# Cross-attention and spectral FFN, one core: one more product per slot from step 56, two blocks' outputs moved, the last context normalised in halves

## The chip, the cores and the metric

The kernel runs on one core of a Trainium2 chip. The metric is the device time of one execution in microseconds (us), median of several runs. Every length of an operation below comes from one profiled execution; times inside it are microseconds from the start of its span.

## The reference

Two batches of 2048 tokens, model width 512, 16 heads of 32, 128 keys of context per batch. What is computed:

```python
q, k, v = decoder_output @ wq_w + wq_b, encoder_output @ wk_w + wk_b, encoder_output @ wv_w + wv_b
score = einsum('bhqd,bhkd->bhqk', q, k) / sqrt(KEY_SIZE) * mask
score = where(score == 0, -1e9, score)
context = softmax(score) @ v                       # heads joined again
x = x + (context @ wo_w + wo_b)                    # q from layernorm(x)
x = x + real(ifft(fft(layernorm(x)) @ w)) + bias   # w complex; here one real 512 x 512 matrix
```

## The kernel before, in words

The 4096 tokens are 16 blocks (c = 0 to 15) of 256 tokens, each of two tiles (t = 0, 1) of 128. All the attention work of a block is cut into four steps s = 4c to 4c+3 of four heads each, 64 steps in all. Weights, queries, contexts and normalised rows are split into a high and a low fp16 part (names ending in h and l), so each 512-wide product is 12 matmuls of 512 columns (high by high, high by low, low by high, four slices each).

Every engine runs one hand-ordered list, and the lists are cut into **slots** v. `plan()` (top of the file) makes TensorE's list. In slot v TensorE (PE) does:

- PT(v-2): the probabilities of step v-2 are transposed (`turn`, L641; 8 transposes, buffers `bank2`, `bank3`), after ScalarE has finished their exponentials (`ex_done`);
- the "mid" products of the slot; WO(c,t) is the attention's output product of tile t of block c (L478, operands `ch`, `cl`), FF(c,t) the FFN product of that tile (L478, operands `x1h`, `x1l`, for block 15 `lasth`, `lastl`);
- S(v+1): the scores of step v+1 (`scores`, L627), which may overwrite the one pair of score banks only when VectorE has read step v (`tt_done`);
- in odd slots PV((v-3)/2): context of two steps (`weigh`, L655); in even ones R((v-4)/2), a "late" fill: the spread reciprocals are turned (L584), after GpSimd's `spread` (L1250, tile `rzb`, semaphore `p_rz`); late products too.

The fills use three PSUM banks in turn (`G[n % 3]`), so a fill waits until VectorE has freed the bank of the third fill before it (`g_free`).

VectorE (DVE) per slot: `mask_mul(v)` (L961, scores times mask), in odd slots `ctx_norm` (L986, context times reciprocal, tile `cn`), `zero_to_neg(v)` (L968, both inputs in SBUF, `eq_done`), `least(v)` (L973, minima), then `lo(n)` for the products: `x <- bank` (L940 after WO, with `bn_stats` L1036 and `bn_aggr` L1041 behind it; L946 after FF). ScalarE (ACT) per slot: in odd slots `copy_rec` (L760, waits for R) first, then half of the exponentials of step v-1 (`exps`, L744, waits for `nbias`), `copy_pt(v-2)` (L753), the other half, and in odd slots `ctx_hi` (L767, `ch` from `cn`). GpSimd (POOL) per slot: it waits for `eq_done` of the slot, then low parts of normalised rows (`norm_lo2`, L1218, `x1nl`), `bias(v)` (L1243, `nbias`, needs `least(v)`; the exponentials wait for it), `ctx_lo` (L1256, `cl`, needs `ch`), `spread` (L1250), `add_bf` (L1229), `add_bo` (L1195), and for blocks 12 and 13 also `norm_hi2` (L1212, `x1nh`), which needs the tile's WO drained by VectorE. `rstd2` (L1202, L1205) is the root for a tile.

FF(c,t) needs `x1h` and `x1l`: the rows `x1nh`, `x1nl` transposed by two DMAs that SyncE (SP) issues (`turn_x1n`, L396) after `p_l2`, the signal of `norm_lo2`. For block 13, tile 1, `norm_lo2` stands in slot 63, ahead of `bias(63)` and behind the wait for `eq_done` of step 63.

After step 63 there is no more softmax: PT63, R30, R31 and PV31 finish block 15's context, `last_ctx_lo` makes its low part, then WO(15,0), WO(15,1), FF(14,0), FF(14,1), FF(15,0), FF(15,1) run (the last in two halves of 256 columns), VectorE adds each, SP stores.

Of the kernel before, what the change touches and what calls it, by code (L numbers as in the profile page):

```python
# [37 lines left out]
def plan():  # L38
# [22 lines left out]
    for v in range(V0, V1):  # L61
# [8 lines left out]
        mid = {NS - 4: [("FF", NC - 4, 0)], NS - 3: [("WO", NC - 3, 1)], NS - 2: [], NS - 1: [("FF", NC - 3, 0)],  # L70
               NS: [("WO", NC - 2, 0)], NS + 1: [("WO", NC - 2, 1)], NS + 2: [("FF", NC - 3, 1)], NS + 3: []}.get(v, mid)
# [57 lines left out]
def build(nc, x, xt, ctx_in, mask, wq, bq, wk, bk, wv, bv, wo, bo, lparts, tables, bf, eye, sums, pick, places, heads, out):  # L129
# [3 lines left out]
    with ExitStack() as stack:  # L133
# [133 lines left out]
        p_l1, p_l2, p_zero, last_cl = (sem(n) for n in ("p_l1", "p_l2", "p_zero", "last_cl"))  # L267
# [410 lines left out]
        def _(act):  # L678
# [136 lines left out]
            for v in range(V0, V1):  # L815
# [55 lines left out]
                if r == 2 and 0 <= c - 2 < NC and v != NS + 2 and c - 2 not in (0, 12, 13):  # L871
                    norm_hi2(c - 2, 1)
                for a in range(4, NC):
                    if hi_slot(a) == v:
                        split_hi(a)
        @block.vector
        def _(dve):
# [207 lines left out]
            for v in range(V0, V1):  # L1085
# [44 lines left out]
                if v == NS - 1:  # L1130
                    tasks += [(stats2, mean2, NC - 3, t) for t in range(2)]
                for n in held + mids:
                    if fills[n][0] == "WO" and fills[n][1] != NC - 3:
# [20 lines left out]
        def _(pool):  # L1154
# [397 lines left out]
```

## Time and profile before

| | us |
|---|---|
| median of 3 runs | 437.13 (437.1 to 437.85) |
| the profiled execution's own time | 437.16 |
| its span, first to last instruction | 435.4 |
| PE busy in the span | 429.1 |
| DVE busy | 398.4 |
| ACT busy | 365.1 |
| POOL busy | 355.6 |
| PE's granted clock | 1.000 of full speed |

The span is what the profile shows; 1.8 us of the execution lie around it. A matmul's row gives its latency (0.38 us for 512 columns), and matmuls of one group start 0.216 us apart, so PE can count as busy while it waits a little: waits are better read from start to start.

### The profile page before, as it was taken

To read this page: it belongs to the slowest core of one execution; us is meant where nothing else is said; L and a number is where in the kernel's file an instruction comes from. 1 tells how busy PE (TensorE), PEld (TensorE's weight loads), DVE (VectorE), ACT (ScalarE), POOL (GpSimd) and SP (SyncE) were. 2 spreads that over 40 slices of the span, in tenths; PEclk is the share of its full clock that TensorE was granted. 3 is DMA by queue.
4 is the path that set the end of the run, shared out by engine and by line. 5 is a ranking of instruction groups with operands and counts; after the bars stand their busy time and mean duration, and the time that the engine had idled before them with its cause. 6 is when DMAs were issued, how large, how long until landed. Compare 5 with 4: busy or idle time off the path is not lost.

```text
span 435.4 us, 10922 instructions
## 1 busy us (share of the span) xinstructions
PE 429.1 (99%) x3496; PEld 297.3 (68%) x3496; DVE 398.4 (92%) x533; ACT 365.1 (84%) x1340; POOL 355.6 (82%) x484
## 2 busy tenths in 40 slices
PE   7999999999999999999999999999999999999997
PEld 6897788686776676666677667766676765556544
DVE  3899799999999999999999999999999899999663
ACT  1768997889988998999898998998998899999720
POOL 5779988868999898989889898989899865665693
PEclk9999999999999999999999999999999999999999
DMA  8999954404545655445454545445542434331144
GB/s 269 396 387 256 305 167 125 107 0 110 128 108 123 168 95 161 102 124 140 128 147 130 132 112 153 92 136 145 110 104 63 108 79 112 75 88 49 50 110 132
DMA packets 85286, 60.15 MB, mean 138 GB/s; under 512 B 40141, under 2 KB 72813, under 8 KB 84718
## 3 DMA queue, kind: packets, MB, share of 16 engines
q1 hardware_dynamic: 84508, 59.29, 50.0%
q8 instruction: 29, 0.48, 0.5%
q10 hardware_dynamic: 722, 0.17, 0.2%
q14 instruction: 27, 0.22, 0.2%
HBM read 29.33 MB, written 8.39 MB: 87 GB/s over the span
## 4 chain that ended last, share of the span: by engine, by line
PE 90%; DVE 4%; POOL 2%; issue 2%; ACT 1%; POOLq 0%; DVEq 0%
PE bank L478 34%; PE bank L483 24%; PE bank L641 11%; PE bank L655 6%; PE scores L627 5%; PE bank L584 3%; PE bank L565 2%; PE scores L483 1%; DVE zs L968 1%; ACT zs L744 1%; PE bank L661 1%; PE bank L491 1%; DVE zs L961 1%; POOL cl L1256 1%; DVE x L946 0%
## 5 line engine op out<-in xcount | busy, mean ns | idle before, releaser
L744 ACT ACTIVATE zs<-zs,nbias 128x128 f32<-128x128 f32 x512 | 199.8, 397 | 13.9 <-POOL nbias L1243 13.5
L744 ACT ACTIVATION_READ_ACCUMULATOR zs<-zs,nbias 128x1 f32 x512 | 99.5, 194 | 0.0
L968 DVE SCALAR_TENSOR_TENSOR zs<-zs 128x1024 f32<-128x1024 f32 x64 | 89.0, 1390 | 1.1
L973 DVE TENSOR_REDUCE nmin<-zs 128x8 f32<-128x1024 f32 x64 | 78.1, 1220 | 2.1
L961 DVE TENSOR_TENSOR zs<-scores,ms 128x1024 f32<-128x1024 f32 x64 | 78.0, 1218 | 0.1
L753 ACT COPY pt<-bank 128x512 f32<-128x512 f32 x128 | 67.9, 582 | 8.2 <-PE bank L641 8.0
L641 PE MATMUL bank<-ident,zs 128*128 128x128 f32 x512 | 66.7, 273 | 0.1
L1195 POOL TENSOR_TENSOR xs<-xs,bob 128x512 f32<-128x512 f32 (+1 forms) x41 | 43.4, 1059 | 22.9 <-DVE zs L968 22.8
L483 PE MATMUL bank<-xth,wqh 128*128 128x256 f16 x224 | 61.2, 273 | 0.0
L483 PE MATMUL bank<-xtl,wqh 128*128 128x256 f16 x224 | 61.1, 273 | 0.0
L483 PE MATMUL bank<-xth,wql 128*128 128x256 f16 x224 | 61.1, 273 | 0.0
L641 PEld LDWEIGHTS bank<-ident,zs 128*128 128x128 f32 x512 | 57.6, 140 | 3.6 <-ACT zs L744 1.7
L478 PE MATMUL bank<-woh,ch 128*128 128x512 f16 x128 | 48.5, 379 | 0.9 <-POOL cl L1256 0.6
L478 PE MATMUL bank<-wol,ch 128*128 128x512 f16 x128 | 48.5, 379 | 0.0
L478 PE MATMUL bank<-woh,cl 128*128 128x512 f16 x128 | 48.5, 379 | 0.0
L478 PE MATMUL bank<-mh,x1h 128*128 128x512 f16 x120 | 45.5, 379 | 0.0
L478 PE MATMUL bank<-ml,x1h 128*128 128x512 f16 x120 | 45.5, 379 | 0.0
L478 PE MATMUL bank<-mh,x1l 128*128 128x512 f16 x120 | 45.5, 379 | 0.0
L1218 POOL TENSOR_TENSOR x1nl<-x,x1nh 128x512 f16<-128x512 f32 x30 | 35.8, 1195 | 9.8 <-DVE zs L968 9.6
L1229 POOL TENSOR_TENSOR x<-x,bfb 128x512 f32<-128x512 f32 x32 | 41.2, 1288 | 1.2 <-DVE zs L968 1.2
L1250 POOL COPY rzb<-rz 128x512 f32<-128x512 f32 x32 | 38.5, 1204 | 2.9 <-DVE rz L979 2.6
L627 PEld LDWEIGHTS scores<-ks,qs 102*128 102x128 f16 (+1 forms) x480 | 31.9, 97 | 13.2 <-issue 0.2
(128 smaller groups left out, 903.9 us busy)
## 6 DMA issues: line engine op xcount, KB each, us to landing
xs<-in_x SPq DMA_DIRECT2D x16, 512.0 KB, 4.3
xtr<-in_xt SPq DMA_DIRECT2D x16, 512.0 KB, 4.6
out<-x SPq DMA_DIRECT2D x31, 256.0 KB, 2.5
qs<-qh SPq DMA_DIRECT2D x120, 64.0 KB
lp<-in_lparts SPq DMA_DIRECT2D x4, 1024.0 KB, 10.3
qs<-ql SPq DMA_DIRECT2D x60, 64.0 KB
ms<-in_mask SPq DMA_DIRECT2D x16, 128.0 KB, 2.5
wks<-in_wk SPq DMA_DIRECT2D x2, 512.0 KB, 6.5
```

Source lines behind the costliest of these rows:

```text
L478: last = pe.matmul(o, a, b, start=(i == 0), stop=(i == len(mm) - 1))
L483: last = pe.matmul(o, a, b, start=(first and i == 0), stop=(i == len(pairs) - 1))
L627: last = pe.matmul(A[:, n % 2, 128 * j:128 * j + 128], qs[c % 2][0:rows, g, j, 128 * t:128 * t + 128], ks[0:rows, g, j, c // (NC // NB), : ...
L641: last = pe.transpose(PB[f][:, a:a + 128], zs[:, s % NZ, t, 2 * f + i, :], ident[:])
L744: last = act.activation(z, z, ACT.Exp, bias=nbias[:, s % 4, i:i + 1], scale=-NEG, accum_out=zsum[:, s % 4, i:i + 1])
L753: act.copy(pt[:, s % 2, 2 * f:2 * f + 2, :], PB[f][:]).then_inc(pt_copied, 1)
L961: dve.tensor_tensor(zs[:, s % NZ], A[:].rearrange("p t (h k) -> p t h k", h=4), ms[:, c % NM].unsqueeze(2).broadcast_to([128, 2, 4, KEYS]) ...
L968: dve.scalar_tensor_tensor(out=z, in0=z, scalar=0.0, in1=z, op0=ALU.is_equal, op1=ALU.subtract).then_inc(eq_done, 1)
L973: dve.tensor_reduce(nmin[:, s % 4, :], zs[:, s % NZ].rearrange("p t h k -> p (t h) k"), AX.X, ALU.min).then_inc(mn_done, 1)
L1195: i = pool.tensor_tensor(z, z, bob[:, n], ALU.add)
L1229: pool.tensor_tensor(z, z, bfb[:], ALU.add).then_inc(p_x1b, 1)
L1250: pool.tensor_copy(rzb[:].rearrange("p i h w -> p (i h) w"), rz[:, z, :].rearrange("p i h -> p (i h)").unsqueeze(2).broadcast_to([128, 16, ...
```

## The change

In the table of mid products (rows 4 of the slots around the end) and in the lists of POOL, DVE and ACT:

- FF(11,0) moves from slot 58 to 56, FF(11,1) from 59 to 58, FF(12,0) from 60 to 59; WO(12,0) becomes a late fill of slot 56. So slot 56 has two products, and slot 60 one less.
- FF(12,1) moves from the end of slot 62 ahead of the scores there. FF(13,1) moves from slot 66 to 64. WO(14,0) moves from 64 to 65, WO(14,1) from 65 to 66. WO(13,0) stays behind the scores of slot 60.
- In the slots 58, 59, 62 and 63 (`BEHIND`) DVE drains the slot's products one slot later, behind the next `least`.
- POOL: block 12's `norm_hi2` and statistics are done as block 13's were; in slot 61 `norm_hi2(13,0)` now stands ahead of `bias(61)`.
- The last context is normalised, cast and subtracted in two halves of 128 tokens (`last_ctx_norm`, `last_ctx_hi`, `last_ctx_lo`; semaphores `last_cn`, `last_ch`, `last_cl`), so WO(15,0) waits for the first half only.

Counts of matmuls, transposes and DMAs are the same.

```diff
+BEHIND = (NS - 6, NS - 5, NS - 2, NS - 1)
...
-        mid = {NS - 4: [("FF", NC - 4, 0)], NS - 3: [("WO", NC - 3, 1)], NS - 2: [], NS - 1: [("FF", NC - 3, 0)],
-               NS: [("WO", NC - 2, 0)], NS + 1: [("WO", NC - 2, 1)], NS + 2: [("FF", NC - 3, 1)], NS + 3: []}.get(v, mid)
+        mid = {NS - 8: [("FF", NC - 5, 0)], NS - 6: [("FF", NC - 5, 1)], NS - 5: [("FF", NC - 4, 0)],
+               NS - 2: [("FF", NC - 4, 1)], NS - 1: [("FF", NC - 3, 0)], NS: [("FF", NC - 3, 1)],
+               NS - 4: [], NS + 1: [("WO", NC - 2, 0)], NS + 2: [("WO", NC - 2, 1)], NS + 3: []}.get(v, mid)
...
-        if v == NS - 4:
-            late.append(("WO", NC - 3, 0))
-        if v == NS - 2:
-            late.append(("FF", NC - 4, 1))
+        if v in (NS - 8, NS - 4):
+            late.append(("WO", v // 4 - 2, 0))
...
+        first = [n for n in held if fills[n][0] in ("R", "ST") and v - 1 not in BEHIND]
+        slots[v] = (items, first, [n for n in held if n not in first],
+                    [n for n in mids if fills[n][0] != "R" and v not in BEHIND])
+        held = mids + lates if v in BEHIND else lates
...
-                    pe.wait_ge(ch_done, 2 * c + 2)
+                    pe.wait_ge(ch_done, min(2 * c + 2, NS // 2 - 1))
                     pe.wait_ge(p_cl, min(2 * c + 2, NS // 2 - 1))
                     if c == NC - 1:
-                        pe.wait_ge(last_cl, 1)
+                        pe.wait_ge(last_ch, f + 1)
+                        pe.wait_ge(last_cl, f + 1)
...
+            def last_ctx_hi():
+                c = NC - 1
+                act.wait_ge(g_done, at["WO", c - 2, 1] + 1)
+                for t in range(2):
+                    g = slice(128 * t, 128 * t + 128)
+                    act.wait_ge(last_cn, t + 1)
+                    act.copy(ch[:, c % 2, 2:4, g], cn[:, :, g]).then_inc(last_ch, 1)
...
                 if v == NS + 1:
+                    copy_rec(NS // 2 - 1)
                     norm_hi2(NC - 2, 0)
-                    copy_rec(NS // 2 - 1)
-                    norm_hi2(NC - 2, 1)
-                    ctx_hi(NS // 2 - 1)
+                    last_ctx_hi()
...
+                if v == NS - 5:
+                    rstd2(NC - 4, 0)
+                    rstd2(NC - 4, 1)
...
-                if v == 57:
+                if v == 61:
                     norm_hi2(c - 2, 0)
                 if 0 <= v < NS:
                     bias(v)
...
-                if v == NS - 3:
+                if v == NS - 7:
                     norm_hi2(c - 2, 0)
-                    spread((v - 3) // 2)
+                if v in (NS - 7, NS - 3):
                     norm_lo2(c - 2, 0)
```

**Place 1: PE's list around slots 58 to 60.** Eleven more matmuls of each product are left out. `ident,zs` is PT, `pt,vs` is PV, `ident,rzb` is R, `mh,x1h` opens an FF, `woh,ch` a WO. Before, from PT56 to WO(13,0):

```order
L641 MATMUL bank<-ident,zs 128x128 x8
L478 MATMUL bank<-mh,x1h 128x512
...
L627 MATMUL scores<-ks,qs_63 128x128 x8
L584 MATMUL bank<-ident,rzb 128x128 x4
L641 MATMUL bank<-ident,zs 128x128 x8
L478 MATMUL bank<-mh,x1h 128x512
...
L627 MATMUL scores<-ks,qs_64 128x128 x8
L655 MATMUL bank<-pt,vs 32x256 x8
L641 MATMUL bank<-ident,zs 128x128 x8
L478 MATMUL bank<-mh,x1h 128x512
...
L627 MATMUL scores<-ks,qs_64 128x128 x8
L584 MATMUL bank<-ident,rzb 128x128 x4
L478 MATMUL bank<-woh,ch 128x512
```

Now, slots 59 and 60, from PT57 to WO(13,0):

```order
L643 MATMUL bank<-ident,zs 128x128 x8
L479 MATMUL bank<-mh,x1h 128x512
...
L629 MATMUL scores<-ks,qs_64 128x128 x8
L657 MATMUL bank<-pt,vs 32x256 x8
L643 MATMUL bank<-ident,zs 128x128 x8
L629 MATMUL scores<-ks,qs_64 128x128 x8
L585 MATMUL bank<-ident,rzb 128x128 x4
L479 MATMUL bank<-woh,ch 128x512
```

The product between PT58 and the scores of step 61 is gone, so S61 and R28 come right behind PT58.

**Place 2: PE's list from PV30 to the product behind PV31.** Before:

```order
L655 MATMUL bank<-pt,vs 32x256 x8
L641 MATMUL bank<-ident,zs 128x128 x8
L478 MATMUL bank<-woh,ch 128x512
...
L584 MATMUL bank<-ident,rzb 128x128 x4
L641 MATMUL bank<-ident,zs 128x128 x8
L478 MATMUL bank<-woh,ch 128x512
...
L584 MATMUL bank<-ident,rzb 128x128 x4
L655 MATMUL bank<-pt,vs 32x256 x8
L478 MATMUL bank<-mh,x1h 128x512
```

Now:

```order
L657 MATMUL bank<-pt,vs 32x256 x8
L643 MATMUL bank<-ident,zs 128x128 x8
L479 MATMUL bank<-mh,x1h 128x512
...
L585 MATMUL bank<-ident,rzb 128x128 x4
L643 MATMUL bank<-ident,zs 128x128 x8
L479 MATMUL bank<-woh,ch 128x512
...
L585 MATMUL bank<-ident,rzb 128x128 x4
L657 MATMUL bank<-pt,vs 32x256 x8
L479 MATMUL bank<-woh,ch 128x512
```

FF(13,1) stood last of these, behind PV31; it is now the first product behind PT62.

**Place 3: POOL's list, slot 61.** Before:

```order
L1243 TENSOR_SCALAR nbias<-nmin 128x8
L1212 CAST x1nh<-x_76 128x512
L1250 COPY rzb<-rz 128x512
L1218 TENSOR_TENSOR x1nl<-x_76,x1nh 128x512
L1256 TENSOR_TENSOR cl<-cn,ch 128x512
```

Now:

```order
L1231 CAST x1nh<-x_76 128x512
L1262 TENSOR_SCALAR nbias<-nmin 128x8
L1237 TENSOR_TENSOR x1nl<-x_76,x1nh 128x512
L1269 COPY rzb<-rz 128x512
L1275 TENSOR_TENSOR cl<-cn,ch 128x512
```

The cast of tile (13,0), which waits for the drain of WO(13,0), is now ahead of `nbias` of step 61.

## Rows read from the trace of the kernel before

**Rows 1.** The page, busy time, share, instructions, all engines.

```profile
PE 429.1 (99%) x3496; PEld 297.3 (68%) x3496; DVE 398.4 (92%) x533; ACT 365.1 (84%) x1340; POOL 355.6 (82%) x484
```

**Rows 2.** PE timeline, slots 56 to 58: start, us, operation, [idle before, releaser].

```profile
363.67 1.09 PE L641 MATMUL bank<-ident,zs 128*128 128x128 f32 x8
365.39 0.38 PE L478 MATMUL bank<-woh,ch 128*128 128x512 f16 x1 [0.63 <-POOL cl L1256]
...
367.98 0.61 PE L627 MATMUL scores<-ks,qs 102*128 102x128 f16 x8
368.43 0.61 PE L584 MATMUL bank<-ident,rzb 128*128 128x128 f32 x4
368.87 1.04 PE L641 MATMUL bank<-ident,zs 128*128 128x128 f32 x8
369.75 0.38 PE L478 MATMUL bank<-woh,ch 128*128 128x512 f16 x1
...
372.33 0.61 PE L627 MATMUL scores<-ks,qs 102*128 102x128 f16 x8
372.88 1.07 PE L655 MATMUL bank<-pt,vs 128*32 128x256 f32 x16
373.88 1.09 PE L641 MATMUL bank<-ident,zs 128*128 128x128 f32 x8
```

**Rows 3.** PE timeline, places where starts lie further apart (slots 59, 65, 66).

```profile
377.85 0.60 PE L584 MATMUL bank<-ident,rzb 128*128 128x128 f32 x4
378.60 1.09 PE L641 MATMUL bank<-ident,zs 128*128 128x128 f32 x8
...
408.67 1.04 PE L641 MATMUL bank<-ident,zs 128*128 128x128 f32 x8
409.87 0.39 PE L478 MATMUL bank<-woh,ch 128*128 128x512 f16 x1 [0.17 <-DVE x L946]
...
416.39 0.38 PE L478 MATMUL bank<-mh,x1l 128*128 128x512 f16 x1
416.89 0.38 PE L478 MATMUL bank<-woh,ch 128*128 128x512 f16 x1
```

**Rows 4.** DVE timeline, step 63's `zero_to_neg`.

```profile
400.58 1.55 DVE L968 SCALAR_TENSOR_TENSOR zs<-zs 128x1024 f32<-128x1024 f32 x1
```

**Rows 5.** POOL and SP timelines behind it, and landings of `x1l` there.

```profile
402.28 1.16 POOL L1218 TENSOR_TENSOR x1nl<-x,x1nh 128x512 f16<-128x512 f32 x1 [1.23 <-DVE zs L968]
...
404.75 1.26 SPq L396 DMA_TRANSPOSE x1l<-x1nl  x1
...
DMA to landing us min/median/max: 2.5/2.5/2.5
```

**Rows 6.** ACT timeline, slot 59 before.

```profile
381.08 1.04 ACT L753 COPY pt<-bank 128x512 f32<-128x512 f32 x2
...
383.58 0.61 ACT L767 CAST ch<-cn 128x512 f16<-128x512 f32 x1
```

**Rows 7.** DVE timeline, slot 59 and the start of 60.

```profile
380.88 0.68 DVE L986 TENSOR_TENSOR cn<-bank,rec 128x512 f32<-128x512 f32 x1
381.48 1.22 DVE L968 SCALAR_TENSOR_TENSOR zs<-zs 128x1024 f32<-128x1024 f32 x1
382.74 1.22 DVE L973 TENSOR_REDUCE nmin<-zs 128x8 f32<-128x1024 f32 x1
383.87 0.74 DVE L946 SCALAR_TENSOR_TENSOR x<-bank,rs,x 128x512 f32<-128x512 f32 x1
...
384.69 1.16 DVE L961 TENSOR_TENSOR zs<-scores,ms 128x1024 f32<-128x1024 f32 x1
```

**Rows 8.** DVE and POOL timeline, `zero_to_neg` meeting POOL's operations.

```profile
198.19 0.73 POOL L1195 TENSOR_TENSOR xs<-xs,bob 128x256 f32<-128x256 f32 x1
198.33 1.67 DVE L968 SCALAR_TENSOR_TENSOR zs<-zs 128x1024 f32<-128x1024 f32 x1
198.85 1.62 POOL L1250 COPY rzb<-rz 128x512 f32<-128x512 f32 x1
```

More of the change, by code:

```diff
@@ L265, in build @@
         dc_done, wz_lo, l0_done, m_hi, m_lo, b_zero, l2_done, o_lo = (sem(n) for n in ("dc_done", "wz_lo", "l0_done", "m_hi", "m_lo", "b_zero", "l2_done", "o_lo"))
[L267 removed]
+        p_l1, p_l2, p_zero, last_cn, last_ch, last_cl = (sem(n) for n in ("p_l1", "p_l2", "p_zero", "last_cn", "last_ch", "last_cl"))
         p_const, p_ms, p_nb, p_cl, p_st, p_xb, p_r2, p_x1b, p_sm, l_done, p_rz = (
@@ L872, in _ @@
                     norm_hi2(c - 2, 1)
+                if v == NS + 2:
+                    norm_hi2(NC - 2, 1)
                 for a in range(4, NC):
@@ L986, in ctx_norm, with last_ctx_norm @@
                 dve.tensor_tensor(cn[:], CX[:].rearrange("p (i n) -> p i n", i=2), rec[:], ALU.mult).then_inc(cn_done, 1)
+            def last_ctx_norm():
+                m = NS // 2 - 1
+                dve.wait_ge(rc_done, m + 1)
+                dve.wait_ge(pv_done, m + 1)
+                dve.wait_ge(p_cl, m)
+                for t in range(2):
+                    g = slice(128 * t, 128 * t + 128)
+                    dve.tensor_tensor(cn[:, :, g], CX[:].rearrange("p (i n) -> p i n", i=2)[:, :, g], rec[:, :, g],
+                                      ALU.mult).then_inc(last_cn, 1)
             def last_ctx_lo():
-                m = NS // 2 - 1
                 c = NC - 1
-                dve.wait_ge(ch_done, m + 1)
-                dve.tensor_tensor(cl[:, c % 2, 2:4, :], cn[:], ch[:, c % 2, 2:4, :], ALU.subtract).then_inc(last_cl, 1)
+                for t in range(2):
+                    g = slice(128 * t, 128 * t + 128)
+                    dve.wait_ge(last_ch, t + 1)
+                    dve.tensor_tensor(cl[:, c % 2, 2:4, g], cn[:, :, g], ch[:, c % 2, 2:4, g],
+                                      ALU.subtract).then_inc(last_cl, 1)
             def split_lo0():
@@ L1119, in _ @@
                         recip(0)
-                    if fills[n][0] not in ("M", "Y") and v != NS - 1:
+                    if fills[n][0] not in ("M", "Y"):
                         lo(n)
@@ L1129, in _ @@
                           if a != 6 and stats_slot(a, t) == v]
[L1130 to L1133, printed above, removed]
+                if v in (NS - 6, NS - 1):
+                    tasks += [(stats2, mean2, NC - 4 + (v == NS - 1), t) for t in range(2)]
+                for n in mids:
+                    if fills[n][0] == "WO" and fills[n][1] not in (NC - 4, NC - 3):
                         tasks.append((stats2, mean2, *fills[n][1:]))
@@ L1136, in _ @@
                     stats(*ct)
-                if v > 3 and v % 2 == 1 and 0 <= v - 3 < NS - 2 and v not in (NS - 3, NS - 1):
+                if v > 3 and v % 2 == 1 and 0 <= v - 3 < NS - 2:
                     recip((v - 3) // 2)
@@ L1330, in _ @@
                     add_bo(15, 0)
-                if r == 1 and 0 <= c - 2 < NC and v not in (13, NS - 3, NS + 1):
+                if r == 1 and 0 <= c - 2 < NC and v not in (13, NS - 7, NS - 3, NS + 1):
                     rstd2(c - 2, 0)
+                if v == NS - 5:
+                    rstd2(NC - 4, 0)
+                    rstd2(NC - 4, 1)
                 if v == NS:
                     rstd2(NC - 3, 0)
-                    rstd2(NC - 3, 1)
                 if v == NS + 2:
@@ L1339, in _ @@
                     rstd2(1, 0)
-                if r == 2 and 0 <= c - 2 < NC and v not in (NS - 2, NS + 2):
+                if r == 2 and 0 <= c - 2 < NC and v not in (NS - 6, NS - 2, NS + 2):
                     rstd2(c - 2, 1)
@@ L1421, in _ @@
                     norm_lo2(c - 2, 1)
-                if v not in (NS - 4, NS + 1) and r < 2 and 0 <= c - 3 < NC and v > 13 and not (r == 1 and VT <= v < NS):
+                if v not in (NS - 8, NS - 4, NS + 1) and r < 2 and 0 <= c - 3 < NC and v > 13 and not (r == 1 and VT <= v < NS):
                     add_bf(c - 3, r)
@@ L1427, in _ @@
                     norm_hi2(c - 2, 1)
+                if v == 56:
+                    add_bo(13, 1)
                 if v == 60:
@@ L1430, in _ @@
                     add_bo(14, 1)
+                if v == NS:
+                    rstd2(NC - 3, 1)
+                    add_bf(NC - 3, 1)
                 if v == 3:
@@ L1445, in _ @@
                     split_lo(3, slice(0, 2), False)
-                if v > VP and v % 2 == 1 and 0 <= v - 3 < NS - 2 and v != NS - 3:
+                if v > VP and v % 2 == 1 and 0 <= v - 3 < NS - 2:
                     spread((v - 3) // 2)
```

22 lines of the change are left out of this document (6 added, 16 removed).

## The prediction

> **What bounds the kernel now.** I read the page first: PE is busy 429.1 of 435.4 us [rows 1], so work of other engines costs nothing unless it makes PE wait. The change leaves PE's work as it is, matmul for matmul, so it can only take waits away or add them. Next I read PE's timeline from start to start. It gives the length of each piece of PE's list [rows 2]: a product takes 2.59 us (365.39 to 367.98), the scores 0.45, or 0.54 ahead of a PV; R 0.44, PV 1.00, and PT 0.88 behind an R (368.87 to 369.75) and 0.93 behind a PV. Wherever the next start comes later than this, PE waited.
>
> Before, these waits are: slot 56, 365.39 - 363.67 - 0.93 = 0.79 for `cl` of POOL [rows 2]; slot 59, 378.60 - 377.85 - 0.44 = 0.31 for exponentials; slot 65, 409.87 - 408.67 - 0.88 = 0.32 for a freed bank; ahead of WO(15,0), 416.89 - 416.39 - 0.22 = 0.28 for the last context's low part [rows 3]. With three of 0.07 to 0.09 that the same reading gives, the waits come to 1.96 us. That is all that can be won here.
>
> **The change part by part.**
>
> *Slot 56.* FF(11,0) fills the wait for `cl`: its transposed rows are there, and it starts at 363.67 + 0.93 = 364.60. Won: 0.79. PE is then one product further in its list than before at each later step, so what the products and fills need must come up to 2.59 us earlier than before relative to it, while the softmax chain on DVE doesn't get faster.
>
> *Slots 57 and 58.* I find nothing late. PE's list to R27 is four products (10.36), three scores (1.44), one R (0.44), one PV (1.00) and PT 0.88 and 0.93: 15.05, so R27 starts at 379.65 (before 377.85 [rows 3]).
>
> *Slot 60.* ACT's first work in slot 59 is to copy R27. That copy starts when R27 is through (0.60 [rows 3]), at about 380.3, and the exponentials of step 58 are queued behind it, though their `nbias` is ready earlier. The copy (0.48 to the next start), four exponentials (2.50 - 0.95 = 1.55) and then the 2.50 from the `pt` copies to `ch` [rows 6] put `ch` of context 27 at 384.8 to 385.4, where before it ran at 383.58. POOL makes `cl` of it in 1.16, 385.5 to 386.66, and only then `rzb` for R28.
>
> By then DVE is at `zero_to_neg(60)`. Block 12's two statistics stand ahead of `mask_mul(59)`, which I place at 379.95. From there: 1.13 to `cn`, 0.60, 1.26, 1.13, then 0.82 to `mask_mul(60)` and 1.2 more [rows 7], so it is issued at 386.1. It meets a running POOL operation, and the trace shows what that costs [rows 8]: the operation on `zs` issued at 198.33 took 1.67, not 1.22, since POOL ran to 198.92 (198.19 + 0.73), and POOL's next operation, issued at 198.85, did not end before 200.47, 0.47 behind DVE's. So DVE ends 1.08 behind POOL's end, at 387.74, and `rzb` at 388.2. PE has done PT58 and S61 by 386.6 and stands at R28 until 388.25. **New wait: 1.6 us**, and 0.07 at S61. This is what was hidden by FF(12,0) between PT58 and S61, which has moved up; there is no other cover. If DVE did not hold `rzb` back, it would be 0.75. I take 1.6, since it is the same two operations that meet in [rows 8].
>
> *Slots 61 to 63.* From 364.60 to S63 lie eight products (20.72), three scores at 0.45 and three at 0.54 (2.97), three R (1.32), three PV (3.00) and PT of 5.43: 33.44, and with 1.67 of waits S63 starts at 399.7. DVE can begin `mask_mul(63)` when the scores are through, 0.6 later, at 400.3; it is ready before that (399.2), so here PE's delay reaches DVE. Then 1.13, 0.60 and 1.22 give the end of `zero_to_neg(63)` at 403.3. Before it was 400.58 + 1.55 = 402.13 [rows 4]. PT61 and PT62 wait for exponentials for about 0.3 together, which drowns in the next wait.
>
> *Slot 64, the main term.* FF(13,1) now comes behind PT62, before it came behind PV31. It needs `x1l` of its tile, and that chain did not move: `x1nl` follows the end of `zero_to_neg(63)` (402.28 behind 402.13), the second transpose is issued at 404.75 and lands 2.5 later, at 407.25 [rows 5]. So **FF(13,1) cannot start before that end plus 5.12**. With 403.3 that is 408.4. PE gets there at about 406.3 by the lengths in [rows 2], so it waits **2.1 us**, with R30, PT63 and all of the tail queued behind FF(13,1).
>
> *The tail.* From FF(13,1) PE has: product 2.59, R 0.44, PT 0.88, WO(14,0) 2.59, R 0.44, PV 1.00, WO(14,1) 2.59, WO(15) 5.18, FF(14) 5.18, FF(15) 5.37, together 26.26 to the end of PE, which was at 432.62. The halves take away the 0.28 ahead of WO(15,0); behind WO(14,1) the half context has 2.59 to be ready and needs some 1.7. The split costs DVE and ACT two short instructions more each, beside PE's product. I cost both at nothing; without the cover it would be some tenths.
>
> *Sum.* 408.4 + 26.26 = 434.7, against 432.62: **+2.1 us**. As a ledger: 1.96 of old waits gone, new ones of 0.07, 1.6, 0.3 and 2.1. What follows PE's end is unchanged. The profiled execution took 437.16 and the median is 437.13, so I forecast 437.13 + 2.1 = **439.2 us**.
>
> *A rule to weigh.* The one fixed price in the main term is the transpose: 2.5 us from issue to landing [rows 5]. The Trainium skill, "VectorE: DVE Perf Modes", section "The three transpose paths", gives 1309 ns for a 128 x 128 16-bit transpose by DMA. By that figure FF(13,1) would start 1.2 us earlier and the sum would be +0.9 instead of +2.1. The row is of this very DMA, which transposes four such tiles, so the row decides.
>
> **The rivals.**
>
> *Faster.* If `zero_to_neg(63)` ended early enough, FF(13,1) would not wait and all old waits would be gone: 437.13 - 1.96 = 435.2. It breaks even when FF(13,1) can start at 432.62 - 26.26 = 406.36, that is when `zero_to_neg(63)` ends by 401.24, 0.9 earlier than before. For it: slot 56 frees DVE of WO(12,0)'s statistics early, so DVE leads by 0.8 in slot 57. Against it: the same drains and statistics stand before step 63 in DVE's list as before, only in other slots, and DVE had hardly any idle time there to lose. Chance 0.08.
>
> *Only the transposes count.* If R28 waits for 0.7 or less, S63 is in time for DVE, and `zero_to_neg(63)` ends between 402.1 and 402.6. FF(13,1) starts at 407.25 to 407.7, and PE ends 0.9 to 1.35 later than before: 438.0 to 438.5. For it: if DVE runs 0.4 earlier in slot 60 it doesn't meet POOL. Chance 0.27.
>
> *The cast ahead of `nbias(61)`.* In POOL's list of slot 61 `x1nh` of (13,0) needs the drain of WO(13,0), which DVE does behind `least(61)`. So `nbias(61)` comes some 1.5 us later behind its minima than before, and the exponentials of step 61 with it. By my count they end at 400.2, with PT61 due at 400.7, so it costs nothing; if ACT runs 1 us later, PT61 and PV30 wait and step 63 with them: +3.1, 440.2. Chance 0.12.
>
> *The change does nothing that shows.* Waits only trade places, within 0.2% of before, which is about what a measurement of this kernel can tell from no change (0.9 us). FF(13,1) would have to wait for less than 2 us beyond what is won. Chance 0.08.
>
> **How the numbers follow.** My forecast has 0.45, with 438.7 to 439.7 as its own range. I let the range reach from the low end of the second rival, 437.9, to the third's, 440.2. Slower by over 0.2% means over 438.0: the forecast, the third rival, and 0.22 of the second, together 0.79. Within 0.2%: 0.05 of the second and the last, 0.13. Faster: 0.08.
>
> **What would show it.** In PE's timeline behind, the matmuls of FF(11,0) start at 364.6 with no gap; R28 starts over 1 us behind S61; the largest gap of the kernel's middle stands ahead of the first `mh,x1h` behind PT62, about 2 us, and ends with the landing of `x1l`, 5.1 behind the end of `zero_to_neg(63)`; no gap ahead of WO(15,0). DVE's `zs` operation of step 60 takes over 1.5. I am wrong if FF(13,1) starts without a gap, if its gap has another releaser, or if `zero_to_neg(63)` ends before 401.3. If R28 doesn't wait but the rest holds, the second rival was right.

## The result and the profile after

| | before | after |
|---|---|---|
| median, us | 437.45 (437.10 to 439.18, 7 runs) | 442.00 (439.70 to 442.84, 7 runs) |
| ratio of the medians, 95% interval | | 1.0087 [1.0068, 1.0105] |
| profiled execution, us | 437.16 | 442.28 |
| its span, us | 435.4 | 440.4 |

The change makes the kernel 0.9% slower, 4.55 us in the medians. I had forecast +2.1 us, and 440.2 as the top of the range: the sign is right, the size is not. The seven executions with the change fall into two groups: 439.70 and 440.11 at a mean granted clock of 1.0, and five from 441.87 to 442.84 at 0.996. Those groups turn out to be half of the answer.

The page of the kernel after, busy times, to set beside [rows 1]:

```profile
PE 430.9 (98%) x3496; PEld 298.4 (68%) x3496; DVE 397.9 (90%) x535; ACT 365.5 (83%) x1341; POOL 359.0 (82%) x484
```

PE has the same 3496 matmuls and is busy 1.8 us longer with them. That is a hint and no more, since this figure moves by itself: the traces below that keep the full clock and the same matmuls show 428.7 to 430.2. What it hints at is a term that my sum lacked.

PE's timeline after, slots 60 and 61, has the first new wait (start, us, operation, [idle before, releaser]):

```profile
385.92 1.09 PE L643 MATMUL bank<-ident,zs 128*128 128x128 f32 x8
387.11 0.62 PE L629 MATMUL scores<-ks,qs 102*128 102x128 f16 x8
389.19 0.63 PE L585 MATMUL bank<-ident,rzb 128*128 128x128 f32 x4 [1.46 <-POOL rzb L1269]
389.65 0.38 PE L479 MATMUL bank<-woh,ch 128*128 128x512 f16 x1
```

R28 starts 2.08 behind S61, where 0.45 is the length of S61 in [rows 2]: PE waits 1.63 (the view counts 1.46, from the end of the last matmul). S61 itself starts 1.19 behind PT58, 0.26 late.

The same engine in slot 64, the second and largest:

```profile
405.22 1.07 PE L657 MATMUL bank<-pt,vs 128*32 128x256 f32 x16
406.55 1.09 PE L643 MATMUL bank<-ident,zs 128*128 128x128 f32 x8 [0.26 <-ACT zs L746]
409.64 0.58 PE L479 MATMUL bank<-mh,x1h 128*128 128x512 f16 x1 [2.00 <-DMA x1l<-x1nl]
410.02 0.63 PE L479 MATMUL bank<-ml,x1h 128*128 128x512 f16 x1
410.44 0.63 PE L479 MATMUL bank<-mh,x1l 128*128 128x512 f16 x1
...
413.00 0.42 PE L479 MATMUL bank<-mh,x1l 128*128 128x512 f16 x1
...
413.91 0.60 PE L585 MATMUL bank<-ident,rzb 128*128 128x128 f32 x4
```

FF(13,1) starts 3.09 behind PT62, 0.93 of which is PT62's own length: it waits 2.16 for `x1l`. Then look at the durations. A matmul of 512 columns takes 0.38 in every row of [rows 2], and here 0.63; starts lie 0.43 apart, not 0.22. FF(13,1) takes 413.91 - 409.64 = 4.27 instead of 2.59, 1.68 more, with nothing to wait for.

The windows view of the kernel after says why. Its columns are the stretch, its length, the busy time of PE, PE's loads, DVE, ACT and POOL with their counts, the granted TensorE clock, the DMA share and GB/s:

```profile
405.00:408.00 3.00, 2.38 (x26) 1.27 (x24) 2.75 (x7) 3.00 (x15) 1.83 (x3) 1.00 0.23 46
408.00:410.00 2.00, 0.36 (x1) 0.14 (x2) 0.00 (x0) 2.00 (x9) 1.66 (x5) 0.92 0.63 181
410.00:411.00 1.00, 1.00 (x4) 0.42 (x3) 0.00 (x0) 1.00 (x6) 1.00 (x1) 0.50 0.17 47
411.00:412.00 1.00, 1.00 (x4) 0.31 (x3) 0.72 (x1) 0.06 (x1) 0.83 (x3) 0.50 0.00 0
412.00:413.00 1.00, 1.00 (x3) 0.29 (x2) 0.03 (x1) 0.00 (x0) 0.83 (x2) 0.50 0.00 0
413.00:414.00 1.00, 1.00 (x6) 0.56 (x5) 0.00 (x0) 0.00 (x0) 0.51 (x1) 0.96 0.00 0
414.00:420.00 6.00, 6.00 (x48) 3.51 (x47) 3.46 (x7) 3.18 (x6) 3.33 (x4) 1.00 0.00 0
```

The granted clock is 0.50 from shortly before 410 to just behind 413: PE ran at 1.2 GHz and not at 2.4, right behind its two idle microseconds. The kernel before shows 1.00 in all of these stretches.

Behind `zero_to_neg(63)` the chain to `x1l` stands as in [rows 4] and [rows 5]. DVE's timeline after:

```profile
401.42 1.23 DVE L972 TENSOR_TENSOR zs<-scores,ms 128x1024 f32<-128x1024 f32 x1 [0.99 <-PE scores L629]
...
403.16 1.22 DVE L979 SCALAR_TENSOR_TENSOR zs<-zs 128x1024 f32<-128x1024 f32 x1
```

POOL's and SP's timelines behind it, and the landings of `x1l` there, as in [rows 5]:

```profile
404.52 1.16 POOL L1237 TENSOR_TENSOR x1nl<-x,x1nh 128x512 f16<-128x512 f32 x1 [1.75 <-DVE zs L979]
...
407.00 1.27 SPq L397 DMA_TRANSPOSE x1l<-x1nl  x1
...
DMA to landing us min/median/max: 2.5/2.5/2.5
```

DVE sits idle 0.99 for the scores of step 63, so PE's delay at R28 did reach DVE. The operation then ends at 404.38, and FF(13,1) starts 5.26 later.

**The ledger.** In the two profiled executions PT54 starts at 363.67 before and 364.49 after. These 0.82 arise ahead of 7.5 us, while PE waits for its first inputs (the ten-matmul group of L661 in the one and L663 in the other starts at 6.47 and at 7.33), and the change doesn't touch that part. From here on I count from PT54's start to the end of PE: 432.62 - 363.67 = 68.95 before, 437.67 - 364.49 = 73.18 after, **4.23 more**. Of these 1.68 are the clock, which leaves 2.55 for the waits, old ones gone and new ones come. This reading leaves out the start-up and can be compared between traces, within a limit that the last experiment shows; I use it for every run below and call it the late part.

### The profile page after: what moved, and what is told of

It reads as the page before. It is cut to its first block, busy times and chain, and to the rows that moved or that the text cites. A ratio compares the mean times of both kernels' runs of the same rounds, so it can differ in the third digit from the quotient of the medians.

```text
span 440.4 us, 10929 instructions
## 1 busy us (share of the span) xinstructions
PE 430.9 (98%) x3496; PEld 298.4 (68%) x3496; DVE 397.9 (90%) x535; ACT 365.5 (83%) x1341; POOL 359.0 (82%) x484
## 4 chain that ended last, share of the span: by engine, by line
PE 71%; DVE 10%; POOL 9%; issue 6%; ACT 2%; DMA 2%; SPq 0%; POOLq 0%; DVEq 0%
PE bank L479 28%; PE bank L484 18%; PE bank L643 8%; PE bank L657 5%; PE scores L629 4%; DVE zs L979 2%; PE bank L566 2%; PE bank L585 2%; DVE zs L972 2%; POOL x L1248 1%; POOL rzb L1269 1%; PE scores L484 1%; POOL x1nl L1237 1%; DVE nmin L984 1%; DMA cxs<-in_ctx 1%
## 5 line engine op out<-in xcount | busy, mean ns | idle before, releaser
L1269 POOL COPY rzb<-rz 128x512 f32<-128x512 f32 x32 | 40.6, 1267 | 1.7 <-DVE rz L990 1.6
```

Of the source, the lines that this page charges most:

```text
L1269: pool.tensor_copy(rzb[:].rearrange("p i h w -> p (i h) w"), rz[:, z, :].rearrange("p i h -> p (i h)").unsqueeze(2).broadcast_to([128, 16, ...
```

## The experiments

The quoted text in each section is what I expected before the run. Each ratio is against the kernel before, timed beside the run: 437.66 (15 runs) for the first four kernels, 437.91 (35 runs) for the rest.

Two theories on the missing two microseconds: (A) the clock fell because PE idled ahead of FF(13,1), so the wait costs its own length and 1.7 more; (B) the slow stretch belongs to something else in that place (the product, the DMA traffic) and would stay if PE were kept busy. And two on the waits themselves: they add up to the end, or the one at R28 is mostly absorbed by the other.

### The wait filled with products

Ten extra products of 512 columns into the bank that FF(13,1) overwrites. They leave the result as it is and start nothing earlier.

```diff
                     pe.wait_ge(m_lo, 4)
+                    if c == NC - 3 and f == 1:
+                        for i in range(10):
+                            pe.matmul(o[:], woh[:, 0, 0:128], woh[:, 1, :], start=True, stop=True)
                     pe.wait_ge(d_t2[f], 32 * (c + 1))
```

> The changed kernel with ten extra matmuls of 512 columns into FF(13,1)'s own bank, between PT62 and the wait for x1l of tile (13,1): 10 x 0.216 = 2.16 us, as long as PE stands idle there now (2.16). Their results are overwritten by FF(13,1). Theory A (the idle wait itself makes the granted clock fall to half for 3.4 us right behind it, which costs 1.7 us): no execution shows a clock under 1.000, FF(13,1) starts when it did (5.1 behind the end of zero_to_neg(63)) and takes 2.6 us, and the time is 439.7 to 440.6. Theory B (the clock falls for another reason, such as the wait at R28 or the sum of waits since slot 60): the clock still shows 0.996 and the time is that of the changed kernel, 442.

Measured: 440.19 (439.90 to 440.44, 5 runs, all at clock 1.0) against 437.66, ratio 1.0055 [1.0042, 1.0069]. PE's timeline of this kernel in slot 64:

```profile
405.97 1.09 PE L646 MATMUL bank<-ident,zs 128*128 128x128 f32 x8 [0.26 <-ACT zs L749]
406.90 2.32 PE L600 MATMUL bank<-woh 128*128 128x512 f16 x10
409.06 0.38 PE L479 MATMUL bank<-mh,x1h 128*128 128x512 f16 x1
```

and its windows there:

```profile
408.00:410.00 2.00, 2.00 (x11) 0.94 (x10) 0.00 (x0) 2.00 (x9) 1.66 (x4) 1.00 0.52 165
410.00:411.00 1.00, 1.00 (x6) 0.42 (x5) 0.29 (x1) 0.48 (x4) 0.83 (x3) 1.00 0.00 0
```

FF(13,1) starts as late as before (409.06 - 363.92 = 45.14 behind PT54, against 45.15), with the same two transposes ahead of it, and now takes 0.38 per matmul at clock 1.00. The late part is 71.50: 2.55 over the kernel before, just what the ledger left for the waits, and 1.68 under the change. **Theory A is shown, B falls:** without the idle stretch the clock doesn't fall. That such a stretch lets it fall each time isn't shown, and isn't so (five of seven executions). This run also is the change without its second fault: +2.53 in the medians, with the forecast of +2.1 beside it.

### FF(13,1) back behind PV31

The main term undone, the rest of the change kept: WO(14,0) and WO(14,1) take slots 64 and 65 again, FF(13,1) slot 66.

```diff
-               NS - 2: [("FF", NC - 4, 1)], NS - 1: [("FF", NC - 3, 0)], NS: [("FF", NC - 3, 1)],
-               NS - 4: [], NS + 1: [("WO", NC - 2, 0)], NS + 2: [("WO", NC - 2, 1)], NS + 3: []}.get(v, mid)
+               NS - 2: [("FF", NC - 4, 1)], NS - 1: [("FF", NC - 3, 0)], NS: [("WO", NC - 2, 0)],
+               NS - 4: [], NS + 1: [("WO", NC - 2, 1)], NS + 2: [("FF", NC - 3, 1)], NS + 3: []}.get(v, mid)
```

> The changed kernel with FF(13,1) back behind PV31, WO(14,0) in slot 64 and WO(14,1) in 65, as before; all the rest of the change stays. Theory A (the wait for x1l is the main loss, R28's wait stays but mostly shifts the softmax chain): no wait for a DMA on PE, clock 1.000, R28 still waits 1.6; PT63 waits some 0.5 for exponentials; PE ends about 0.9 later than before: 438.0 to 438.5. Rival (the order of the tail is not what costs, DVE's later chain is): the time stays within 1 us of the changed kernel, over 441.

Measured: 439.18 (438.32 to 441.19, 9 runs), ratio 1.0034 [1.0021, 1.0047]; eight executions at clock 1.0, and the one of 441.19 at 0.996. The median missed the expected 438.0 to 438.5 by 0.7. The late part is 70.25, +1.30 where I expected +0.9, and 1.25 better than the filled kernel at the same clock. The 2.16 are gone, but PE is again first at a door. Its timeline in slot 64:

```profile
406.12 1.09 PE L643 MATMUL bank<-ident,zs 128*128 128x128 f32 x8 [0.26 <-ACT zs L746]
407.96 0.38 PE L479 MATMUL bank<-woh,ch 128*128 128x512 f16 x1 [0.75 <-POOL cl L1275]
```

WO(14,0) waits 0.91 (1.84 - 0.93) for `cl`, because PE is a product ahead of its suppliers there as well. I had expected 0.5 of waiting at PT63 instead, where there is none: that is the 0.4 by which I missed in the late part.

### `rzb` of R28 ahead of `cl` on POOL

The other wait taken away: in its slot 59, while PE is in slot 60, POOL spreads the sums of context 28 ahead of the subtraction of context 27, so that nothing late stands in front of `rzb`.

```diff
                 elif v % 2 == 1 and 2 <= v - 5 < NS - 2:
+                    if v == NS - 5:
+                        spread((v - 3) // 2)
                     ctx_lo((v - 5) // 2)
...
-                if v > VP and v % 2 == 1 and 0 <= v - 3 < NS - 2:
+                if v > VP and v % 2 == 1 and 0 <= v - 3 < NS - 2 and v != NS - 5:
```

> The changed kernel with spread(28) (the tile rzb for R28) ahead of ctx_lo(27) in POOL's slot 59. The wait at R28 (1.63 us in the changed kernel) goes. Theory A (that wait reaches the end only through mask_mul(63), which waited 0.99 us for S63; from there on the chain eq(63), x1nl, transposes, FF(13,1) sets the end): PE's wait ahead of FF(13,1) grows to about 3.0 us, the low clock stays, and only 0.7 us are won: 441.3 to 441.6. Rival (PE's waits add up): 1.6 us are won, 440.4.

Measured: 440.79 (439.71 to 441.18, 6 runs, two at clock 1.0 and four at 0.996), ratio 1.0065 [1.0052, 1.0079]. That lies between the two expectations, 441.3 to 441.6 and 440.4, and the times don't decide: at 0.996 the median of four is 440.98, 1.3 under that of the change's five, while the two at 1.0, 439.71 and 440.27, are no faster than the change's two, 439.70 and 440.11. So I go by the trace. The profiled execution had clock 1.0, although PE waits longer in it than in the change, so it compares with the filled kernel. POOL's timeline of this kernel there:

```profile
385.82 0.61 POOL L1269 COPY rzb<-rz 128x512 f32<-128x512 f32 x1
386.39 1.17 POOL L1275 TENSOR_TENSOR cl<-cn,ch 128x512 f16<-128x512 f32 x1
```

PE's in slots 60 to 64:

```profile
386.89 0.62 PE L629 MATMUL scores<-ks,qs 102*128 102x128 f16 x8
387.35 0.61 PE L585 MATMUL bank<-ident,rzb 128*128 128x128 f32 x4
...
400.94 1.09 PE L643 MATMUL bank<-ident,zs 128*128 128x128 f32 x8 [0.79 <-ACT zs L746]
...
408.83 0.38 PE L479 MATMUL bank<-mh,x1h 128*128 128x512 f16 x1 [2.19 <-DMA x1l<-x1nl]
```

R28 no longer waits. But the late part is 70.92, only 0.58 better than the filled kernel's 71.50. PE spends the rest of the 1.63 elsewhere, 0.98 of it ahead of PT61, and its wait ahead of FF(13,1) grows to 2.35. **In this trace the wait at R28 was mostly absorbed.** What sets FF(13,1) is the end of `zero_to_neg(63)`, which this edit moves from 39.88 to 39.31 behind PT54, by 0.57. The scores of step 63 come 1.65 earlier; DVE takes up 1.13 of that and gives half of the 1.13 back. POOL's and DVE's timelines of this kernel show where:

```profile
401.88 0.62 POOL L1231 CAST x1nh<-x 128x512 f16<-128x512 f32 x1
```
```profile
400.07 1.22 DVE L972 TENSOR_TENSOR zs<-scores,ms 128x1024 f32<-128x1024 f32 x1
...
401.99 1.59 DVE L979 SCALAR_TENSOR_TENSOR zs<-zs 128x1024 f32<-128x1024 f32 x1
```

`mask_mul(63)` starts 35.80 behind PT54, 1.13 sooner than after the change (401.42 - 364.49 = 36.93). Then `zs` is issued while POOL casts `x1nh` and takes 1.59 instead of 1.22 (0.17 more went ahead of `cn`): its end, 403.58, is 1.08 behind POOL's 402.50, the very distance that the prediction took from [rows 8]. My sum has R28 only through S63 and DVE, so it did not add the 1.6 to the end; the ledger line "1.6" was easily read as a price of its own, and it isn't one.

The new 0.98 ahead of PT61 has a cause of its own, the third rival's: in slot 61 POOL casts `x1nh` of (13,0) ahead of `nbias`. POOL's and ACT's timelines of this kernel there:

```profile
395.76 0.61 POOL L1231 CAST x1nh<-x 128x512 f16<-128x512 f32 x1 [3.06 <-DVE nmin L984]
396.46 0.23 POOL L1262 TENSOR_SCALAR nbias<-nmin 128x8 f32<-128x8 f32 x1
```
```profile
396.73 0.40 ACT L746 ACTIVATE zs<-zs,nbias 128x128 f32<-128x128 f32 x1 [1.61 <-POOL nbias L1262]
```

The minima of step 61 end at 395.04, so `nbias` comes 1.42 behind them; in the kernel before it comes 0.15 behind them (393.65 against 393.50), and ACT stands idle 1.61 for it. With the change as it is, the wait at R28 hides this order. No run changes it alone on a kernel with `rzb` first.

### FF(13,1) begins with what is there

The eight matmuls of `x1h` first, behind a wait for `x1h` alone, then the four of `x1l`. The first transpose of that tile gets a semaphore of its own.

```diff
-                    pe.wait_ge(d_t2[f], 32 * (c + 1))
+                    if c == NC - 3 and f == 1:
+                        pe.wait_ge(d_h13, 16)
+                        for k in range(4):
+                            pe.matmul(o[:], x1h[:, f, k, :], mh[:, k, :], start=(k == 0), stop=False)
+                            pe.matmul(o[:], x1h[:, f, k, :], ml[:, k, :], start=False, stop=False)
+                        pe.wait_ge(d_t2[f], turned(c + 1, f))
+                        for k in range(4):
+                            last = pe.matmul(o[:], x1l[:, f, k, :], mh[:, k, :], start=False, stop=(k == 3))
+                        last.then_inc(g_done, 1)
+                        return
+                    pe.wait_ge(d_t2[f], turned(c + 1, f))
```

> The changed kernel with FF(13,1)'s 12 matmuls in another order: the eight that read x1h wait for the first transpose alone, the four that read x1l come last. x1h lands 1.25 us ahead of x1l, and eight matmuls take 1.73. Theory A: PE's wait falls from 2.16 to about 0.9 and the clock does not fall: 442.3 - 1.25 - 1.7 = 439.3, between 438.7 and 440. Rival (another resource is just as late, the landing is no bound): the clock recovers, but the wait of PE reappears at R30 or PT63 and the time stays over 440.5.

Measured: 439.31 (438.88 to 440.19, 6 runs, clocks of 0.999 and 1.0), ratio 1.0038 [1.0024, 1.0051].

```profile
408.51 0.38 PE L607 MATMUL bank<-mh,x1h 128*128 128x512 f16 x1 [0.66 <-DMA x1h<-x1nh]
...
415.56 0.63 PE L591 MATMUL bank<-ident,rzb 128*128 128x128 f32 x4 [0.40 <-POOL rzb L1287]
```

The wait is 0.82 (408.51 - 406.76 - 0.93) and no execution shows 0.996. The late part is 70.76, 0.74 better than the filled kernel; I had expected 1.25, and the difference is a new wait of 0.56 ahead of R31. Again a supplier is late as soon as PE is not. The median is the expected one.

### Both waits undone

FF(13,1) back and `rzb` first, the two edits above together.

> The two edits of e2 and e3 together: FF(13,1) behind PV31 and spread(28) ahead of ctx_lo(27). e2's PE waits were 1.63 at R28, 0.9 at WO(14,0) for cl, 0.33 and 0.26. Theory A (DVE's softmax chain, not PE's sum, sets the end from slot 61 on): R28's wait goes, but only 0.6 us reach the end as in e3; 438.4 to 438.8, PE's end 0.6 to 0.8 later than before against the same start of slot 56. Rival (the waits add up): 1.6 less than e2, 437.5.

Measured: 438.39 (437.80 to 438.94, 12 runs) against 437.91, ratio 1.0009 [0.9996, 1.0022]. The late part is 69.40, +0.45, a little better than the 0.6 to 0.8 that I expected. Against the kernel with only FF(13,1) back, `rzb` first is worth 0.85 of the 1.63 here (0.79 in the medians), where it was worth 0.58 above. With all that the change was told to bring in place (no wait in slot 56, none ahead of WO(15,0)) and both of its large new waits gone, it still isn't faster. Its timeline shows where the rest went:

```profile
399.83 0.63 PE L585 MATMUL bank<-ident,rzb 128*128 128x128 f32 x4
401.26 0.98 PE L643 MATMUL bank<-ident,zs 128*128 128x128 f32 x7 [0.80 <-ACT zs L746]
...
407.65 0.38 PE L479 MATMUL bank<-woh,ch 128*128 128x512 f16 x1 [0.68 <-POOL cl L1275]
```

0.99 ahead of PT61 for the exponentials, 0.84 ahead of WO(14,0) for `cl`, 0.26 ahead of S61: 2.1, and with four of 0.05 to 0.14 together 2.5, for the 1.96 that the kernel before spends. The 0.99 comes again behind the cast ahead of `nbias(61)` (ACT idles 1.53 for it), so whether this kernel with the old POOL order in slot 61 would be faster than before stays open.

### The halves alone

The kernel before, with only the last context's `cn`, `ch` and `cl` made in two halves and WO(15,0) waiting for the first.

> The kernel before with the last context in halves and nothing else. Both theories: the 0.28 ahead of WO(15,0) goes and nothing comes in its place; 0.3 us faster than before, which the timing can hardly tell; in PE's timeline FF(13,1) to WO(15,0) falls from 2.88 to 2.6. If the split costs more than it gives (two more instructions on DVE and ACT), the wait stays over 0.2.

Measured: 437.53 (436.90 to 439.92, 12 runs), ratio 0.9998 [0.9980, 1.0015]. In the trace WO(15,0) starts 2.60 behind the first matmul of the product ahead of it, as it should without a wait:

```profile
414.99 0.39 PE L478 MATMUL bank<-mh,x1h 128*128 128x512 f16 x1
...
417.59 0.38 PE L478 MATMUL bank<-woh,ch 128*128 128x512 f16 x1
```

The late part is 68.74, 0.21 less than before, for the 0.28 that [rows 3] give. The mechanism shows in the trace; in the times 0.2 us can't be told from nothing.

### Another order: WO(12,0) one slot piece later

An attempt to win slot 56 without running ahead of DVE later. PE's table is that of the kernel before, but WO(12,0), which waited for `cl` in slot 56, goes behind S57 and R26 of the same slot, and no other product moves. Halves and the change's other lists are kept, `nbias(61)` ahead of the cast. The lines are against the kernel before.

```diff
-        mid = {NS - 4: [("FF", NC - 4, 0)], NS - 3: [("WO", NC - 3, 1)], NS - 2: [], NS - 1: [("FF", NC - 3, 0)],
-               NS: [("WO", NC - 2, 0)], NS + 1: [("WO", NC - 2, 1)], NS + 2: [("FF", NC - 3, 1)], NS + 3: []}.get(v, mid)
+        mid = {NS - 8: [], NS - 7: [("WO", NC - 4, 1)], NS - 6: [("FF", NC - 5, 0)], NS - 5: [("FF", NC - 5, 1)],
+               NS - 4: [("FF", NC - 4, 0)], NS - 2: [], NS - 1: [("FF", NC - 3, 0)], NS: [("WO", NC - 2, 0)],
+               NS + 1: [("WO", NC - 2, 1)], NS + 2: [("FF", NC - 3, 1)], NS + 3: []}.get(v, mid)
...
-        if v == NS - 4:
-            late.append(("WO", NC - 3, 0))
+        if v in (NS - 8, NS - 4):
+            late.append(("WO", v // 4 - 2, 0))
```

> PE's order of before, with one product moved by two small pieces: WO(12,0) stands behind the scores and R of slot 56 (0.89 us of other work) instead of ahead of them, with the changed kernel's halves and its POOL and DVE lists for block 12; nbias(61) ahead of x1nh(13,0) as before. Theory A (the wins of 0.79 and 0.28 can be had without bringing any FF nearer to its transposes): no wait at the first WO of slot 56, R28 waits less than 0.3, no DMA on PE's waits; 1.0 us faster than before, 436.4 to 436.9. Rival (DVE's chain sets slots 56 to 63 anyway): PE's wait reappears ahead of PT57 to PT61 and the time is that of before.

Measured: 437.42 (437.09 to 438.85, 12 runs), ratio 0.9988 [0.9975, 1.0002], where I had expected 436.4 to 436.9. The old waits are gone and two new ones stand in their place, both for DVE:

```profile
363.70 1.09 PE L645 MATMUL bank<-ident,zs 128*128 128x128 f32 x8
365.54 0.62 PE L631 MATMUL scores<-ks,qs 102*128 102x128 f16 x8 [0.74 <-DVE zs L974]
...
388.77 0.39 PE L481 MATMUL bank<-woh,ch 128*128 128x512 f16 x1 [0.71 <-DVE x L959]
```

0.91 ahead of S57, for the score banks, and 0.88 ahead of WO(13,0), for a freed bank. The late part is 68.93, as before.

### The same order with FF(13,1) in slot 64

The main term alone, on the kernel just above, which has no wait at R28. The lines are against that kernel.

```diff
-               NS - 4: [("FF", NC - 4, 0)], NS - 2: [], NS - 1: [("FF", NC - 3, 0)], NS: [("WO", NC - 2, 0)],
-               NS + 1: [("WO", NC - 2, 1)], NS + 2: [("FF", NC - 3, 1)], NS + 3: []}.get(v, mid)
+               NS - 4: [("FF", NC - 4, 0)], NS - 2: [], NS - 1: [("FF", NC - 3, 0)], NS: [("FF", NC - 3, 1)],
+               NS + 1: [("WO", NC - 2, 0)], NS + 2: [("WO", NC - 2, 1)], NS + 3: []}.get(v, mid)
```

> e7 with FF(13,1) in slot 64 ahead of R30 and WO(14,0), WO(14,1) one slot later, that is the change's main move alone. Theory A: FF(13,1) starts 5.1 behind the end of zero_to_neg(63), which is where it was before (402.1 with slot 56 at 363.67), so PE waits 1 to 1.8 us there; 1 to 1.6 us slower than e7 at full clock, and in some executions 1.7 more with a granted clock of 0.996. Rival (the wait in the changed kernel came from the late DVE chain alone): wait under 0.5, within 0.4 us of e7.

Measured: 439.15 (437.97 to 439.94, 12 runs), ratio 1.0022 [1.0007, 1.0037], 1.73 over the kernel just above, a little over the 1 to 1.6 that I expected.

```profile
405.48 1.09 PE L645 MATMUL bank<-ident,zs 128*128 128x128 f32 x8
408.07 0.38 PE L481 MATMUL bank<-mh,x1h 128*128 128x512 f16 x1 [1.50 <-DMA x1l<-x1nl]
```

The wait is 2.59 - 0.93 = 1.66, and it starts 5.25 behind the end of `zero_to_neg(63)` (401.26 + 1.56 = 402.82). Counted from PT59, the first piece of slot 61, to the end of PE it is 42.91 here and 41.26 in the kernel just above, 1.65 more: with R28 unhindered, this edit by itself costs what the wait is long. No execution of the twelve shows 0.996.

The late part, though, is 69.93, only 1.00 more. The 0.65 between the two readings lies in slots 56 to 60, where the two kernels have the same lists: the wait ahead of WO(13,0) is 0.88 in the one trace and 0.24 in the other. DVE's timelines show the largest piece of it, `zero_to_neg(58)` in the kernel just above and in this one:

```profile
374.78 1.70 DVE L981 SCALAR_TENSOR_TENSOR zs<-zs 128x1024 f32<-128x1024 f32 x1
```
```profile
375.57 1.22 DVE L981 SCALAR_TENSOR_TENSOR zs<-zs 128x1024 f32<-128x1024 f32 x1
```

In the first POOL's `rzb` is issued at 374.79 and takes 0.61, and DVE is the one that takes longer; in the second both are issued at 375.57, DVE takes 1.22 and `rzb` 1.69. The same code gives either. `zero_to_neg(60)` adds 0.19 (1.59 against 1.40). So a late part of one trace can move by some 0.65 for no edit where such operations meet. The four traces with the change's lists up to slot 63 don't: PT62 starts 42.05 to 42.07 behind PT54 in each.

## Why the prediction was right or wrong

| step | predicted | after, by the profile |
|---|---|---|
| FF(11,0) fills slot 56's wait | starts at 364.6, 0.79 won | 365.42, 0.93 behind PT54, no wait |
| S61, R28 late | 0.07, 1.6 | 0.26, 1.63 |
| `zs` of step 60 meets POOL | over 1.5, end 387.74 | 1.49, end 388.57 (387.75 with the start-up's 0.82 taken off) |
| end of `zero_to_neg(63)` | 403.3 | 404.38 (403.56) |
| from there to FF(13,1) | 5.12 | 5.26 |
| start of FF(13,1) | 408.4 | 409.64 (408.82) |
| its wait | 2.1 | 2.16 |
| WO(15,0) | no wait | none |
| from FF(13,1) to the end of PE | 26.26 | 28.03 |
| sum | +2.1 | +4.23 (+2.55 with PE kept busy) |

**Right:** each wait that the text named stands where it named it, with the releaser it named. Slot 60 went as told, and `rzb` after `cl` is what holds R28. POOL's timeline after, while PE is in that slot, the rows that answer to [rows 8]:

```profile
386.33 1.16 POOL L1275 TENSOR_TENSOR cl<-cn,ch 128x512 f16<-128x512 f32 x1 [0.41 <-ACT ch L769]
387.44 1.61 POOL L1269 COPY rzb<-rz 128x512 f32<-128x512 f32 x1
```

and DVE's:

```profile
387.08 1.49 DVE L979 SCALAR_TENSOR_TENSOR zs<-zs 128x1024 f32<-128x1024 f32 x1
```

`zs` takes 1.49 and not 1.22 while POOL still works at `cl`, and `rzb`, 0.61 in the run that put it first, takes 1.61 here and ends 0.48 behind DVE's 388.57; the forecast used 0.47. Of the rivals, the second fell with R28's 1.63, and the third's cast cost nothing, PT61 starting 0.44 behind R29; but the experiments show that it was only hidden. The Trainium skill, "GPSIMD Engine Reference", section 1, has GpSimd share its SBUF interfaces with VectorE where a VectorE instruction has two SBUF inputs; these rows agree, with 1.0 us more for `rzb`.

**Mis-sized:** the waits, by 0.45. `zero_to_neg(63)` came 0.26 later than I had it, since S61 waited 0.26 and not 0.07 and R28 1.63 and not 1.6; 0.14 passed between the landing of `x1l` and PE's first matmul, which "end plus 5.12" left out, and 0.09 is the wait ahead of PV31, which stands in both traces and which the 26.26 left out. The filled run measured this part by itself: +2.55. Two executions of the change that kept their clock, 439.70 and 440.11, lie inside the range.

**Wrong:** the step "the tail". It costed the 26.26 behind FF(13,1) from rows of a busy PE, as if a 2 us gap ahead of them changed nothing. The profiled tail took 28.03, 1.68 of it FF(13,1) itself at 1.2 GHz. I had no rival for this either: all of them took PE's durations as fixed. The granted clock stood on the page that I read first, but the kernel before keeps PE at 99%, and nowhere in the stretch that I read does its clock fall; a change that makes the first gap of 2 us was the very case in which to ask what the clock would do. With this term priced at either level, from 0 to 1.7, the top of the range would have stood at 441.9 instead of 440.2, beside a median of 442.0. That the two executions at full clock lie inside the range says that the waits were nearly right; which clock the median would show I had not asked.

The Trainium skill, "TensorE: Matmul & The Clock Gate", Part 1, says that an idle TensorE is given every second pulse, 1.2 GHz, and the full clock after it has been busy again. The windows above agree with both levels, 0.50 and 1.00. I had not weighed this page in the prediction.

**The rule that I weighed** against the row, 1309 ns for the transpose by the Trainium skill, "VectorE: DVE Perf Modes", section "The three transpose paths": the row decided rightly. Issue to landing is 2.5 us after the change too, and an estimate by the page's figure for one tile of 128 x 128 gives FF(13,1) a wait of some 1.0 instead of 2.16.

**Start-up:** 0.82 of the 5.12 between the two profiled executions lies ahead of anything that the change touches and isn't part of its price; in the medians it shows as spread.

**No gain in any order.** Of the orders of slots 56 to 66 that the runs timed, none beats the kernel before by what can be measured: the best is 437.42 against 437.91, with 1 in the interval of the ratio. That interval reaches down to 0.9975, so a gain of a microsecond isn't excluded either. In the traces each order removes most of the 1.96 us of old waits and gets as much or more of others: `rzb`, `cl`, exponentials, a freed bank. DVE is busy 92% of the span [rows 1], and its pace may be what lies behind these waits, but that is argued and not shown; nor is it shown that no order does better, only that these don't. The order with both large waits undone and `nbias(61)` ahead of the cast was not run. What else stays open: why the clock fell in five of seven executions and not in all, why it stayed in the one trace with a wait of 2.35, and which wait did it in the one execution of the kernel with FF(13,1) back that shows 0.996.

## What to carry to other kernels

Before moving a consumer earlier, count from the last operation of its slowest supplier chain (here vector operation, cast, transpose, landing: 5.26 us) to the place where the consumer will stand; if that is later than TensorE arrives, the wait is real however many other waits the move removes. Price a new TensorE gap of about 2 us twice, with the clock kept and with the next product at half clock, and put both in the range. Where several waits lie on one chain, undo them one at a time at the same clock: 1.63 us at R28 were worth 0.58 at the end in one pair of traces and 0.85 in another. And compare two traces only from a point up to which both ran alike, since the same code gave 0.65 more or less.

## What the runs showed of the hardware that I had not expected

- **The clock fell after a gap of about 2 us.** By kernel, with the wait ahead of slot 64's product in its profiled execution: filled, 0 of 5 executions at 0.996; 0.82 us, 0 of 6; 0.84, 0 of 12; 0.91, 1 of 9; 1.66, 0 of 12; 2.16 (the change), 5 of 7; 2.35, 4 of 6, and not in the very execution in which the 2.35 was read. In the change's profiled execution the half clock begins just behind the wait, lasts 3.4 us by the windows (3.0 at 0.50 and the two stretches at 0.92 and 0.96 beside them), and costs 1.68. What decides in which executions it falls, these runs don't show.
- **The same kernel at two speeds.** With the change, executions at 1.0 and at 0.996 differ by 1.8 to 3.1 us. Its median says little until they are told apart by the granted clock.
- **A delay that works in both directions.** `rzb` of R28 took 0.61 ahead of `cl` and 1.61 where it met DVE's `zs`; the `zs` operation takes 1.22 alone, and 1.49 and 1.59 where POOL was at work when it was issued. Where both are issued within 0.01 us, either can be the one that takes longer: DVE's 1.70 beside an `rzb` of 0.61, or DVE's 1.22 beside an `rzb` of 1.69, from the same code.
